# Cross attention of a two-layer decoder: the first query projection and the first key-value tile change places in TensorE's order

## The chip, the cores and the metric

One core of one Trainium2 chip. The metric is the device time of one execution in microseconds (us), as the median of several runs. The trace is that of one profiled execution on the same core.

## The reference, cut to what matters

The program computes a decoder of two layers on a float32 activation `x` of 8 sequences, 256 tokens each, 256 features. Each layer adds to `x` an attention, a second attention and an expert stage, each behind a layer norm. The change concerns the second layer's cross attention alone: 16 query heads, 4 key-value heads, head size 128, a context of 64 tokens per sequence.

```python
q = rms_norm(x @ Wq.T, q_norm_w)                # 16 heads, 256 tokens
kv_in = concatenate([x, ctx], axis=1)           # 256 + 64 = 320 rows
k = rms_norm(kv_in @ Wk.T, k_norm_w)            # 4 key heads
v = kv_in @ Wv.T
q, k = rope(q, pos_q), rope(k, pos_kv)
probs = softmax(q @ k.T * HD**-0.5)             # k, v shared by 4 query heads
x = x + (probs @ v) @ Wo.T
```

## The kernel before, in words

The program runs its stages one behind the other, each in its own block, with the engines' orders written out by hand and semaphores between them. `attention` (from L258) is used twice: for the first layer's self attention (`cross` false) and for the second layer's cross attention (`cross` true).

A unit of work is one key-value head with its four query heads on one sequence. There are 16 units for each of two buffer sets h = 0 and 1, so 32 in all. A unit goes through two halves. The front half projects queries (two tiles of 128 tokens, `project_q`, L386 to L394) and keys and values (three tiles in the cross attention: two of 128 tokens and one of the 64 context rows, `project_kv`, L396 to L404), rotates them, takes their RMS norms, and transposes the queries and keys (`turn_qk`). The back half computes scores of four heads (`score`), their softmax, transposes the probabilities (`turn_probs`), multiplies them with the values (`mix`) and projects back (`give`). A call of `stage(h, front, back)` runs the front half of a unit in set h beside the back half of a unit in the other set, g = 1 - h. `schedule` issues a first stage with no back half, 31 stages with both, and a last one with no front half. Every engine has its own `stage` function, and the order of calls in it is that engine's order of work.

TensorE's order (L464 to L496) in the cross attention is: first query projection; scores of heads 0 and 1; second query projection and key-value tile 0; transposes of probabilities 0 and 1; mixes 0 and 1; scores 2 and 3; key-value tiles 1 and 2; transposes 2 and 3; mixes 2 and 3; `give`; `turn_qk`. Each PSUM set has four banks: the query tiles of a front half take banks 0 and 1, the key-value tiles 2 and 3.

The waits around the change: `score` of head 0 waits for `qk_kept`, which ScalarE signals after copying the transposed queries (`qT`, L657) and keys (`kT`, L658) out of PSUM. `project_q` of tile 0 waits for GpSimd's copy of the input tokens (L358, L360) and for VectorE's add of the previous output (L604). Three signals on `projected` tell VectorE that query tile 0, query tile 1 and all key-value tiles are there.

VectorE's order (L607 to L636): maxima of heads 0 and 1 (L570), normalization of 0 and 1 (L584, L587), copies of a part of the transposed probabilities (L596), rotation of the query tiles (L522 to L524), maxima 2 and 3, normalization of head 2, rotation of the keys (L522 to L524 again), normalization of head 3, two copies, sums of squares (L550, L551), the add of the rotated halves (L540), scaling of the keys (L558, L562), output add (L604). ScalarE's order (L683 to L702): exponentials (L666), copies of transposed probabilities (L673), copies of mixes (L681), and in `keep_v`, once the keys are rotated, squares (L648 to L650) and values (L652, L653), and last `qT` and `kT`. GpSimd takes the inverse root (L366) and the input copies for the next unit. There are no transfers inside the attention.

The self attention runs `project_q` of tile 0 behind scores 0 and 1, and has two key-value tiles, both behind scores 2 and 3.

Of the kernel before, what the change touches and what calls it, by code (L numbers as in the profile page):

```python
# [257 lines left out]
def attention(k, weights, rope, ctx):  # L258
# [9 lines left out]
    cross = ctx is not None  # L268
    scale = float(HD) ** -0.5
    KT = TB + 1 if cross else TB  # L270
# [5 lines left out]
    with ExitStack() as st:  # L276
# [45 lines left out]
        HB = B // 2  # L322


        early = 1 if cross else 0

        def group(u):
            return u // HB
# [16 lines left out]
        def wait_before(eng, sem, value):  # L345

            if not isinstance(value, int) or value > 0:
                eng.wait_ge(sem, value)

        with nc.Block() as block:  # L350
# [32 lines left out]
            def _(pe):  # L383
                pe.wait_ge(weights.loaded, 16 * weights.loads)

                def project_q(h, u, t):  # L386
                    if t == 0:
                        pe.wait_ge(s.xb_ready[h], u + 1)

                        wait_before(pe, s.out_added[h], u)  # L390
                    for c in range(DC):
                        last = nc.tensor.matmul(k.ps[h][:, t, :], xb[h][:, c, t * P:(t + 1) * P],  # L392
                                                wq[:, c, ds(group(u) * (G * HD), G * HD)], start=c == 0, stop=c == DC - 1)
                    last.then_inc(s.projected[h], 1)  # L394

                def project_kv(h, u, tiles):  # L396
                    for t in tiles:
                        o = k.ps[h][0:krows[t], 2 + t // 2, (t % 2) * 2 * HD:(t % 2 + 1) * 2 * HD]
                        for c in range(DC):
                            last = nc.tensor.matmul(o, xb[h][:, c, t * P:t * P + krows[t]],  # L400
                                                    wkv[:, c, ds(group(u) * (2 * HD), 2 * HD)],
                                                    start=c == 0, stop=c == DC - 1)
                    if t == KT - 1:
                        last.then_inc(s.projected[h], 1)  # L404

                def turn_qk(h, u):

                    pe.wait_ge(s.turned_in[h] if cross else s.summed[h], u + 1)
                    pe.wait_ge(s.v_kept[h], u + 1)
                    for hh in range(G):  # L410
                        for t in range(TB):
                            nc.tensor.transpose(slot(h, hh)[:, t * P:(t + 1) * P], t1[h][:, t, hh, :], k.ident[:, :])
                    for t in range(KT):
                        r = krows[t]
                        last = nc.tensor.transpose(k.ps[h][:, 2, t * P:t * P + r], t1[h][0:r, t, G, :],
                                                   k.ident[0:r, 0:r])
                    last.then_inc(s.qk_turned[h], 1)

                def score(h, u, r):
                    if r == 0:  # L420
                        pe.wait_ge(s.qk_kept[h], u + 1)
                    elif r > 1:

                        pe.wait_ge(s.mix_kept[h], u * G + (r - 1))
                    for t in range(TB):
                        nk = NK if cross else (t + 1) * P
                        o = k.ps[h][:, (r % 2) * TB + t, :]
                        last = nc.tensor.matmul(o[:, 0:nk], qT[h][:, r, t * P:(t + 1) * P],  # L428
                                                kT[h][:, 0:nk], start=True, stop=cross)
                        if not cross:  # L430

                            last = nc.tensor.matmul(o[:, t * P:nk], k.identb[:, :],
                                                    k.causb[:, :], start=False, stop=True)
                    last.then_inc(s.scored[h], 1)

                def turn_probs(h, u, r):
                    pe.wait_ge(s.probs_ready[h], u * G + (r + 1))
                    for j in range(KT):
                        w = krows[j]
                        for t in range(TB):  # L440
                            if cross or j <= t:
                                last = nc.tensor.transpose(slot(h, (r % 2) * 4 + pieces[j])[0:w, t * P:(t + 1) * P],  # L442
                                                           probs[h][:, (r % 2) * TB + t, j * P:j * P + w], k.ident[:, :])
                    last.then_inc(s.probs_turned[h], 1)

                def mix(h, u, r):
                    pe.wait_ge(s.probs_kept_a[h], u * G + (r + 1))
                    pe.wait_ge(s.probs_kept_d[h], u * G + (r + 1))
                    for j in range(KT):
                        w = krows[j]  # L450
                        c0 = 0 if cross else j * P
                        last = nc.tensor.matmul(slot(h, (r % 2) * 4 + 3)[:, c0:S], v[h][0:w, j, :],  # L452
                                                pT[h][0:w, r % 2, j, c0:S], start=j == 0, stop=j == KT - 1)
                    last.then_inc(s.mixed[h], 1)

                def give(h, u):
                    pe.wait_ge(s.mix_kept[h], u * G + G)
                    for t in range(TB):
                        for hh in range(G):
                            last = nc.tensor.matmul(slot(h, t), oT[h][:, hh, t * P:(t + 1) * P],  # L460
                                                    wo[:, ds(group(u) * G + hh, 1), :], start=hh == 0, stop=hh == G - 1)
                    last.then_inc(s.out_ready[h], 1)

                def stage(h, front, back):  # L464
                    g = 1 - h
                    if front is not None and cross:
                        project_q(h, front, 0)
                    if back is not None:
                        score(g, back, 0)
                        score(g, back, 1)  # L470
                    if front is not None:
                        if not cross:
                            project_q(h, front, 0)
                        project_q(h, front, 1)
                        if early:
                            project_kv(h, front, range(early))
                    if back is not None:
                        turn_probs(g, back, 0)
                        turn_probs(g, back, 1)
                        mix(g, back, 0)  # L480
                        mix(g, back, 1)
                        score(g, back, 2)
                        score(g, back, 3)
                    if front is not None:
                        project_kv(h, front, range(early, KT))
                    if back is not None:
                        turn_probs(g, back, 2)
                        turn_probs(g, back, 3)
                        mix(g, back, 2)
                        mix(g, back, 3)  # L490
                    if back is not None and cross:
                        give(g, back)
                    if front is not None:
                        turn_qk(h, front)
                    if back is not None and not cross:
                        give(g, back)  # L496
# [1906 lines left out]
def build(nc, ins, out):  # L2403
    with ExitStack() as stack:
        k = Core(nc, ins, out, stack)
        load_constants(k)
        with ExitStack() as st, k.own_semaphores("_0"):
            rope = SelfRope(k, st)
            weights = AttentionWeights(k, ("w0q", "w0kv", "w0o"), st)
            layernorm(k)  # L2410
            attention(k, weights, rope, None)
        layernorm(k)
        with ExitStack() as st, k.own_semaphores("_m"):
            weights = ExpertWeights(k, st)
            set_attention(k)
            routed_experts(k, weights)
        layernorm(k)
        with k.own_semaphores(""):
            delta_attention(k)
        with ExitStack() as st, k.own_semaphores("_1"):  # L2420
            weights = AttentionWeights(k, ("w1xq", "w1xkv", "w1xo"), st)
            rope = CrossRope(k, st)
            layernorm(k)
            attention(k, weights, rope, rope)
        with ExitStack() as st, k.own_semaphores(""):
            k.xn_rows = k.sb("xn_rows", [P, NT, D], F32, st)
            layernorm(k, k.xn_rows)
            sparse_experts(k)
# [83 lines left out]
```

## Time and profile before

| | |
|---|---|
| median of 3 runs | 4484.63 us (4478.69 to 4495.13) |
| profiled execution, its own time | 4505.4 us |
| its span in the trace | 4503.6 us |
| granted TensorE clock over the span | 0.896 |
| busy: TensorE, VectorE, ScalarE, GpSimd | 3543.0, 2730.2, 1614.0, 1555.6 us |

The profile is a page and a packed trace of one execution. Engines: PE is TensorE's matmuls (a transpose is one too), PEld its weight loads, DVE VectorE, ACT ScalarE, POOL GpSimd. A float32 matmul shows as two instructions. The ends of matmuls are modelled, so successive starts are the safer measure of their pace. Lines of the trace such as L428 are lines of the kernel. In the order of time the cross attention lies at about 3050 to 3970 us.

### The profile page before, as it was taken

The page shows a single profiled execution, that of the slowest core. Times are in us where ns is not written, and L with a number is a line of the kernel's source. Part 1 is how long each engine was busy: PE and PEld are TensorE (multiplying, and loading weights), DVE is VectorE, ACT ScalarE, POOL GpSimd, SP SyncE. Part 2 cuts the span into 40 slices and gives each one's busy share as a digit, 9 for nine tenths or more (in the row PEclk, how much of TensorE's full clock was granted, in tenths as well). Part 3 has the DMA queues.
Part 4 walks back from the last instruction along what each step waited for, and adds up shares of the span by engine and source line. Part 5 has one row for each costly group of instructions (what it writes and reads, how often), then busy time and mean ns, then how long its engine had stood idle before and what let it go on. Part 6 is the DMA issues. An engine that isn't in the chain of part 4 may idle for free. (4 is left out here: it accounts for less than half of the span.)

```text
span 4503.6 us, 58245 instructions
## 1 busy us (share of the span) xinstructions
PE 3543.0 (79%) x17574; PEld 2742.3 (61%) x17574; DVE 2730.2 (61%) x7933; ACT 1614.0 (36%) x4118; POOL 1555.6 (35%) x2243
## 2 busy tenths in 40 slices
PE   6999993589577999999999999847999999940320
PEld 4677662455366888888888888735655655530320
DVE  4666652532257888888888888545666666652123
ACT  2434441123234545555555555313444444410100
POOL 0000000058515555555555555501111111117357
PEclk9999995589778999999999999978999999965665
DMA  2000004135411111111111111110000000021340
GB/s 69 0 0 0 0 0 106 63 61 84 85 30 34 29 38 24 38 24 38 28 37 41 24 38 24 19 56 1 0 0 0 0 0 0 0 91 39 100 116 13
DMA packets 225351, 152.21 MB, mean 34 GB/s; under 512 B 125496, under 2 KB 211702, under 8 KB 224096
## 3 DMA queue, kind: packets, MB, share of 16 engines
q1 hardware_dynamic: 192880, 113.99, 9.8%
q0 software_dynamic: 27456, 30.91, 3.7%
q10 hardware_dynamic: 4800, 4.72, 0.3%
q8 instruction: 100, 1.64, 0.1%
q14 instruction: 115, 0.94, 0.1%
HBM read 117.41 MB, written 56.11 MB: 39 GB/s over the span
## 5 line engine op out<-in xcount | busy, mean ns | idle before, releaser
L1869 DVE SCALAR_TENSOR_TENSOR dl_y<-ps,dl_taps,dl_y 128x255 f32<-128x255 f32 (+2 forms) x1536 | 653.0, 475 | 130.6 <-ACT dl_y L1765 126.4
L1600 PE MATMUL ps<-xnT,dl_wkqv 128*128 128x256 f32 x2048 | 544.8, 392 | 29.0 <-DVE dl_lp L1912 23.3
L1600 PEld LDWEIGHTS ps<-xnT,dl_wkqv 128*128 128x128 f32 x2048 | 370.4, 194 | 81.2 <-issue 38.2
L366 POOL TENSOR_TENSOR at_rs<-at_ss,mhalf 128x15 f32<-128x15 f32 x32 | 125.5, 3921 | 745.8 <-DVE at_ss L553 745.8
L1523 POOL TENSOR_TENSOR dl_rn<-dl_n,mhalf 128x4 f32<-128x4 f32 x128 | 173.3, 1354 | 553.0 <-DVE dl_n L1885 553.0
L452 PE MATMUL ps<-at_shared,at_v 128*128 128x256 f32 (+2 forms) x1280 | 315.7, 380 | 4.6 <-ACT at_shared L676 0.2
L1765 ACT ACTIVATE dl_y<-ps,dl_taps 128x256 f32<-128x256 f32 x512 | 260.2, 560 | 106.2 <-PE ps L1600 106.2
L428 PE MATMUL ps<-at_kT,at_qT 128*128 128x320 f32 (+2 forms) x1024 | 271.2, 397 | 2.8 <-ACT at_kT L658 2.8
L1541 POOL TENSOR_TENSOR dl_inv_u<-dl_inv_u,dl_inv_tmp 64x30 f32<-64x30 f32 (+14 forms) x480 | 259.0, 540 | 37.6
L452 PEld LDWEIGHTS ps<-at_shared,at_v 128*128 128x128 f32 (+1 forms) x1280 | 211.1, 190 | 89.3 <-issue 64.0
L392 PE MATMUL ps<-at_wq,at_xb 128*128 (+1 forms) x512 | 246.1, 614 | 4.5 <-POOL at_xb L360 2.4
L442 PE MATMUL ps<-ident,at_probs 128*128 128x128 f32 (+1 forms) x1152 | 173.8, 283 | 96.3 <-DVE at_probs L587 93.1
L460 PE MATMUL ps<-at_wo,at_oT 128*128 (+1 forms) x1024 | 234.8, 382 | 18.7 <-ACT at_oT L681 18.7
L1625 PE MATMUL ps<-dl_wo,dl_z 128*128 128x256 f32 x1024 | 243.2, 380 | 0.0
L1538 POOL TENSOR_TENSOR dl_inv_tmp<-dl_inv_u,dl_inv_a 64x30 f32<-64x30 f32 (+14 forms) x480 | 232.9, 485 | 24.7
L358 POOL COPY at_xb<-xnT 128x512 f32 (+1 forms) x64 | 38.9, 609 | 566.5 <-PE ps L400 561.7
L1773 ACT ACTIVATE dl_z<-dl_y 128x512 f32<-128x512 f32 x256 | 161.5, 631 | 185.2 <-DVE dl_y L1869 185.2
L442 PEld LDWEIGHTS ps<-ident,at_probs 128*128 128x128 f32 (+1 forms) x1152 | 124.1, 135 | 169.5 <-DVE at_probs L587 156.3
L1611 PE MATMUL ps<-dl_z 128*128 128x512 f32 (+1 forms) x512 | 225.4, 523 | 0.0
L460 PEld LDWEIGHTS ps<-at_wo,at_oT 128*128 128x128 f32 x1024 | 189.4, 190 | 54.7 <-issue 27.5
L428 PEld LDWEIGHTS ps<-at_kT,at_qT 128*128 128x128 f32 x1024 | 175.1, 191 | 70.8 <-ACT at_kT L658 13.7
L570 DVE TENSOR_REDUCE at_mx<-ps 128x2 f32<-128x640 f32 x128 | 105.6, 825 | 180.6 <-PE ps L428 177.1
(332 smaller groups left out, 7944.7 us busy)
## 6 DMA issues: line engine op xcount, KB each, us to landing
dl_grow<-decay_rows SPq DMA_DIRECT2D x128, 128.0 KB, 3.0
sp_wgu<-in_w1gu SPq DMA_DIRECT2D x12, 768.0 KB, 10.5
dl_wkqv<-in_w1kqv SPq DMA_DIRECT2D x16, 512.0 KB, 4.9
delta_diag<-dl_lp SPq DMA_DIRECT2D x512, 8.0 KB, 1.5
dl_diag<-delta_diag_tt SPq DMA_DIRECT2D x512, 8.0 KB, 1.7
moe_wgu<-in_w0gu SPq DMA_DIRECT2D x16, 448.0 KB, 10.4
slot_rows<-sp_zero SPq DMA_DIRECT2D x4, 1152.0 KB, 8.1
sp_wd<-in_w1d SPq DMA_DIRECT2D x12, 384.0 KB, 12.0
```

What stands on the lines that cost most here:

```text
L392: last = nc.tensor.matmul(k.ps[h][:, t, :], xb[h][:, c, t * P:(t + 1) * P], wq[:, c, ds(group(u) * (G * HD), G * HD)], start=c == 0, stop= ...
L428: last = nc.tensor.matmul(o[:, 0:nk], qT[h][:, r, t * P:(t + 1) * P], kT[h][:, 0:nk], start=True, stop=cross)
L442: last = nc.tensor.transpose(slot(h, (r % 2) * 4 + pieces[j])[0:w, t * P:(t + 1) * P], probs[h][:, (r % 2) * TB + t, j * P:j * P + w], k.i ...
L452: last = nc.tensor.matmul(slot(h, (r % 2) * 4 + 3)[:, c0:S], v[h][0:w, j, :], pT[h][0:w, r % 2, j, c0:S], start=j == 0, stop=j == KT - 1)
L460: last = nc.tensor.matmul(slot(h, t), oT[h][:, hh, t * P:(t + 1) * P], wo[:, ds(group(u) * G + hh, 1), :], start=hh == 0, stop=hh == G - 1)
L1538: nc.gpsimd.tensor_tensor(tmp, inv_u[:, 0:i, i:i + 1].to_broadcast([GP, i, w]), inv_a[:, i:i + 1, i + 1:Q32].to_broadcast([GP, i, w]), ALU ...
L1541: nc.gpsimd.tensor_tensor(inv_u[:, 0:i, i + 1:Q32], inv_u[:, 0:i, i + 1:Q32], tmp, ALU.subtract)\
L1600: last = nc.tensor.matmul(bank(h, m // 2, (m % 2) * S, (m % 2 + 1) * S), wkqv[h][:, c, m * P:(m + 1) * P], k.xnT[:, c, u.seq * S:(u.seq + ...
L1611: last = nc.tensor.matmul(bank(h, blk, 0, 2 * (S - blk * P)).rearrange("p (a s) -> p a s", a=2), z[h][:, 0, blk * P:(blk + 1) * P], z[h][: ...
L1625: last = nc.tensor.matmul(bank(h, 3, t * D, (t + 1) * D), z[h][:, 2 + m, t * P:(t + 1) * P], wo[h][:, m, :], start=m == 0, stop=m == 1)
L1765: last = nc.scalar.activation(y[h][:, m, :], bank(h, m // 2, (m % 2) * S, (m % 2 + 1) * S), ACT.Identity, bias=taps[h][:, m, KC:KC + 1], s ...
L1869: last = nc.vector.scalar_tensor_tensor(y[h][:, m, back:S], bank(h, m // 2, (m % 2) * S, (m % 2 + 1) * S - back), taps[h][:, m, KC - 1 - b ...
```

## The change

```diff
@@ -322,7 +322,6 @@
         HB = B // 2


-        early = 1 if cross else 0

         def group(u):
             return u // HB
@@ -463,17 +462,12 @@

                 def stage(h, front, back):
                     g = 1 - h
-                    if front is not None and cross:
-                        project_q(h, front, 0)
                     if back is not None:
                         score(g, back, 0)
                         score(g, back, 1)
                     if front is not None:
-                        if not cross:
-                            project_q(h, front, 0)
+                        project_q(h, front, 0)
                         project_q(h, front, 1)
-                        if early:
-                            project_kv(h, front, range(early))
                     if back is not None:
                         turn_probs(g, back, 0)
                         turn_probs(g, back, 1)
@@ -482,7 +476,7 @@
                         score(g, back, 2)
                         score(g, back, 3)
                     if front is not None:
-                        project_kv(h, front, range(early, KT))
+                        project_kv(h, front, range(KT))
                     if back is not None:
                         turn_probs(g, back, 2)
                         turn_probs(g, back, 3)
```

In the cross attention's TensorE order both query projections now stand behind the scores of heads 0 and 1, and all three key-value tiles behind those of heads 2 and 3. The instructions are the same in kind and number, the waits and signals too. The self attention's order stays as it was, and is now the same as the cross attention's up to `give`. The other engines' orders are not touched.

## Rows read from the trace of the kernel before

**Rows 1.** The page, part 2: TensorE's granted clock in 40 slices, in tenths.
```profile
PEclk9999995589778999999999999978999999965665
```

**Rows 2.** Windows: start:end, length, busy us (instructions) of each engine, granted clock.
```profile
3103.00:3950.00 847.00, 771.52 (x3330) 507.65 (x3328) 532.17 (x1410) 356.00 (x931) 140.59 (x88) 1.00 0.00 0
```

**Rows 3.** Source L657 in the cross attention: ns min/median/max, first and last start.
```profile
L657 ACT COPY at_qT<-ps x32: 1012/1012/1012, 3072.7 to 3949.6; 128x1024 f32<-128x1024 f32 x32
```

**Rows 4.** Waits of TensorE, 3074 to 3949.9 us: total, times, longest.
```profile
PE ps L442 <- DVE at_probs L587: 55.5, 93, 1.1
PE ps L460 <- ACT at_oT L681: 17.8, 31, 0.6
PE ps L412 <- DVE at_t L562: 2.8, 16, 0.2
```

**Rows 5.** Timeline of TensorE in a steady stage: start us, busy us, instruction, idle before.
```profile
3528.01 2.32 PE L428 MATMUL ps<-at_kT,at_qT 128*128 128x320 f32 x8
3530.16 1.88 PE L392 MATMUL ps<-at_wq,at_xb 128*128 x4
3531.88 1.03 PE L400 MATMUL ps<-at_wkv,at_xb 128*128 x4
3532.74 0.82 PE L442 MATMUL ps<-ident,at_probs 128*128 128x128 f32 x6
3533.83 0.87 PE L442 MATMUL ps<-ident,at_probs 128*128 128x128 f32 x6 [0.26 <-DVE at_probs L587]
3534.54 3.34 PE L452 MATMUL ps<-at_shared,at_v 128*128 128x256 f32 x12
3537.81 2.42 PE L428 MATMUL ps<-at_kT,at_qT 128*128 128x320 f32 x8
3540.07 2.03 PE L400 MATMUL ps<-at_wkv,at_xb 128*128 x8
3542.53 0.88 PE L442 MATMUL ps<-ident,at_probs 128*128 128x128 f32 x6 [0.43 <-DVE at_probs L587]
3544.50 0.87 PE L442 MATMUL ps<-ident,at_probs 128*128 128x128 f32 x6 [1.10 <-DVE at_probs L587]
```

**Rows 6.** Timeline of ScalarE in the same stage.
```profile
3526.30 1.01 ACT L657 COPY at_qT<-ps 128x1024 f32<-128x1024 f32 x1 [5.57 <-PE ps L415]
...
3533.60 0.59 ACT L673 COPY at_shared<-ps 128x512 f32<-128x512 f32 x1 [0.75 <-PE ps L442]
...
3543.93 1.03 ACT L648 ACTIVATE at_shared<-ps 128x1024 f32<-128x1024 f32 x1
```

**Rows 7.** Timeline of VectorE in the same stage.
```profile
3529.29 0.82 DVE L570 TENSOR_REDUCE at_mx<-ps 128x2 f32<-128x640 f32 x1 [3.72 <-PE ps L428]
...
3541.79 0.68 DVE L587 TENSOR_SCALAR at_probs<-at_probs,at_rden 128x320 f32<-128x320 f32 x2
3542.39 0.42 DVE L522 TENSOR_TENSOR at_t<-ps,rope_ck 128x256 f32<-128x256 f32 x1
...
3543.45 0.21 DVE L524 TENSOR_TENSOR at_t<-ps,rope_sc 64x64 f32<-64x64 f32 x1
...
3543.76 0.68 DVE L587 TENSOR_SCALAR at_probs<-at_probs,at_rden 128x320 f32<-128x320 f32 x2
```

**Rows 8.** Timeline of the last stage, which has no front half.
```profile
3949.55 1.01 ACT L657 COPY at_qT<-ps 128x1024 f32<-128x1024 f32 x1 [5.20 <-PE ps L415]
...
3950.95 2.42 PE L428 MATMUL ps<-at_kT,at_qT 128*128 128x320 f32 x8 [1.43 <-ACT at_kT L658]
3952.33 0.82 DVE L570 TENSOR_REDUCE at_mx<-ps 128x2 f32<-128x640 f32 x1 [3.28 <-PE ps L428]
```

**Rows 9.** Timeline of the first stage, no back half: all key-value tiles in one block.
```profile
3057.01 2.90 PE L400 MATMUL ps<-at_wkv,at_xb 128*128 128x256 f32 x12
...
3059.95 0.42 DVE L522 TENSOR_TENSOR at_t<-ps,rope_ck 128x256 f32<-128x256 f32 x1 [1.38 <-PE ps L400]
```

**Rows 10.** Timeline of the second stage's start: a query projection at the lower clock.
```profile
3072.60 3.72 PE L392 MATMUL ps<-at_wq,at_xb 128*128 128x512 f32 x4
```

## The prediction

> **What bounds the kernel now.** The page comes first: in its 40 slices of 113 us TensorE is granted nearly its full clock through most of this attention, slices 29 to 35 [rows 1]. The windows view of the cross attention's steady part shows TensorE busy for 771.5 of 847.0 us, VectorE 532.2, ScalarE 356.0, at clock 1.00 [rows 2]. So TensorE's queue is the thing to follow, and its idle time is what an order of work can win or lose. The 32 copies of `qT` run from 3072.7 to 3949.6, so a stage takes (3949.6 - 3072.7)/31 = 28.29 us [rows 3]; the sampled steady stage takes 28.24 by the same copy. The waits of TensorE name three kinds of idle time: on normalized probabilities 55.5 us in 93 waits (1.79 a stage), on the kept mix 17.8, on the scaled keys 2.8 [rows 4]. The change moves work around the first kind.
>
> I follow one stage on a clock that starts at T, the start of the `qT` copy at 3526.30 [rows 6]. TensorE's steps [rows 5]: first query projection before T; first scores T+1.71; second query projection T+3.86; key-value tile 0 T+5.58; first transposes of probabilities T+6.44, second T+7.53 (0.26 idle); mixes T+8.24; second scores T+11.51; key-value tiles 1 and 2 T+13.77; third transposes T+16.23 (0.43 idle); fourth T+18.20 (1.10 idle, the largest).
>
> The last wait is a chain through VectorE, to be read in its own rows [rows 7]. It normalizes head 2 from 3541.79, goes straight on to rotate the keys at T+16.09, and only behind that normalizes head 3 from 3543.76. TensorE's fourth transposes wait for that. Whatever delays the key rotation delays head 3's probabilities.
>
> **Part 1: the first query projection goes from ahead of scores 0 and 1 to behind them.** Nothing is added or removed in number: 4 matmuls, no transfer, no new wait. Its two waits (input ready, output added) move with it and were met by its old place. What it loses is its cover. Today it runs while ScalarE copies `qT` and `kT`, which the scores need. The last stage of this attention has no front half, so the trace already shows that stretch without a projection: TensorE idles 1.43 us and scores start 1.40 after the `qT` copy (3950.95 - 3949.55) [rows 8]. Today it is 1.71, so scores start 0.31 sooner. Not all is gain: with no matmul ahead of them their own first one isn't overlapped, and the row maximum starts at T+2.78 there (3952.33 - 3949.55) against T+2.99 today (3529.29 - 3526.30) [rows 7, 8]. I take 0.20 sooner for what follows, so the projections start at T+3.66.
>
> A page bears on a longer gap. The row shows the 8 scores behind the 1.43 us gap taking 2.42 us, the same as scores elsewhere at full clock took with the 0.10 of start-up [rows 5, 8], so I add nothing. The Trainium skill (TensorE: Matmul & The Clock Gate, "Why this matters for your kernels") warns that idle gaps between bursts of matmuls send the clock back to its lower level; by the row this gap doesn't, and if it did the sum would be that of the fourth case below.
>
> **Part 2: key-value tile 0 goes from behind the second query projection to behind scores 2 and 3.** Between scores and first transposes there are now two query projections instead of one and a key-value tile. One query projection takes 3531.88 - 3530.16 = 1.72; tile 0 takes 3532.74 - 3531.88 = 0.86 [rows 5]. First transposes: 3.66 + 2 x 1.72 = T+7.10, 0.66 later than today. Both heads' probabilities are ready before that (they let today's second transposes go at T+7.53, and come 0.2 sooner), so the 0.26 idle is gone. Second transposes follow after 0.71 (the space from transposes to mix today, 3534.54 - 3533.83): T+7.81. The mixes could start at T+8.52, but need ScalarE's copy of the first transposes, which starts 0.86 after them (3533.60 - 3532.74) and takes 0.59 [rows 5, 6]; with 0.06 for the hand-over that is T+8.61, 0.37 later than today. Without the copy it would be 0.28. I take 0.37, since by its own rows the copy ends last, if narrowly.
>
> Scores 2 and 3 and their maxima shift by 0.37; the key-value block now starts at 13.77 + 0.37 = T+14.14, and holds 12 matmuls for 8. The attention's very first stage runs just this block of 12 at full clock: VectorE's key rotation starts 3059.95 - 3057.01 = 2.94 after it begins [rows 9]. So the rotation starts at 14.14 + 2.94 = **T+17.08 instead of T+16.09: 0.99 later**. Head 2 is normalized by T+16.54 (16.17, the end of the two operations from 3541.79, plus 0.37), so VectorE now waits some 0.5 us for tile 0, where before it had no wait at all. Queued behind it: the rotation, head 3's normalization, the last copies, the sums of squares, the adds. TensorE's third transposes start at about T+16.7, 0.5 later, and that is covered; the fourth wait for head 3 and start at T+19.19.
>
> **The tail.** After that every queue carries the 0.99. ScalarE's squares start at 3543.93, 0.28 after the rotation's end (0.21 us operation begun at 3543.45, in the same stretch), since a copy is ahead of them [rows 6, 7]; they slip 0.7 to 0.8, which VectorE's sums, already 0.99 late, hide. GpSimd's inverse root starts from those sums and sets the scaled keys; the TensorE wait on them is small [rows 4], so output projection and key chain are level and both late. No slack there to give anything back. No queue of SyncE or of transfers is passed.
>
> **Sum.** 31 stages have both halves (32 copies less the first stage, whose order stays; the last stage has no projections): 31 x 0.99 = +30.7 us. The same by TensorE's idle time: +1.43 at the start, -0.26 and -0.43 at transposes, more than today's 1.10 at the fourth. Against the profiled execution of 4505.4 us that gives 4536; it is 20.8 above the median of the runs shown, 4484.6, to which I add the same: **4515 us**, +0.68%. About 0.5% is what a measurement of this kernel can tell from no change, 22.4 us or 0.72 a stage.
>
> Bounds of the uncertain terms, per stage: hand-over and copy 0.28 to 0.45; start of scores gain 0.1 to 0.31; block to rotation 2.9 to 3.0. Together 0.8 to 1.15, so 25 to 36 us.
>
> **Rivals.**
> *The delay at the fourth transposes is absorbed.* Only TensorE's balance up to the mixes counts, 0.37 x 31 = 11.5: 4496 us. For it: 1.10 of idle sits in front of the fourth transposes, and TensorE itself is late by only 0.5 there. Against: that idle is VectorE's, queued behind the very rotation that moves.
> *Not slower: stalls removed exceed the one made.* The 1.79 a stage on probabilities [rows 4] all vanish behind longer blocks, and 1.43 appears [rows 8]: -0.36 x 31 = -11, 4473 us. It decides if VectorE's rotation can still start by T+16.09, that is if the key-value block ends nearly 1 us sooner than I have it. Only idle time that I haven't seen inside TensorE's stream could give that.
> *Cover lost in full.* The stalls on probabilities all stay, because scores, maxima and exponentials move with the shift, and the start gap comes whole: 1.43 x 31 = 44: 4529 us.
> *The clock falls in the new gap.* At the lower level of 1.2 GHz the four projection matmuls took 3.72 us at 3072.60 [rows 10] against 1.88 [rows 5], 1.84 more; once a stage, 57 us above the forecast: 4572. The scores of rows 8 speak against it.
>
> **Numbers.** Forecast 0.76, absorbed 0.12, not slower 0.04, cover lost 0.06, clock 0.02. The forecast's own range with 5 to 8 us of scatter between runs is 4503 to 4526; reaching a little towards 4496 and 4529 gives 4500 to 4527. Slower by over 0.5%: 0.84 of cases, less what scatter around 22.4 may take from the forecast, 0.79. Within: 0.19. Faster: the -11 case is -0.25% and would need scatter as well, 0.02.
>
> **What the changed profile would show.** Right: the `qT` copies 29.2 us apart; TensorE waiting about 1.4 us for `kT` in each stage; first and second transposes with no idle; a new VectorE wait of some 0.5 us on the key-value matmuls ahead of the key rotation; fourth transposes waiting 1.4 to 1.6 instead of 1.10; self attention and all other stages unchanged. Wrong: spacing under 28.9, or no VectorE wait before the rotation, or matmuls longer at a lower granted clock.

## The result and the profile after

The changed kernel takes 4528.23 us in the median of 4 runs (4522.94 to 4532.68). The kernel before, with one more run beside it, takes 4489.88 (4478.69 to 4495.35). The ratio is 1.009, with a 95% interval of 1.0075 to 1.0105: slower by 34 to 47 us, where 30.7 were forecast and the range ended at 4527.

The first view is the one that gave the length of a stage: the copies of `qT` (rows 3 before; here also those of the self attention, so the last start is the one to read) and the timeline of the cross attention's first, last and two steady ones.

```profile
L651 ACT COPY at_qT<-ps x32: 1012/1012/1012, 3066.0 to 3982.2; 128x1024 f32<-128x1024 f32 x32
...
3127.26 1.01 ACT L651 COPY at_qT<-ps 128x1024 f32<-128x1024 f32 x1 [5.57 <-PE ps L414]
3156.55 1.01 ACT L651 COPY at_qT<-ps 128x1024 f32<-128x1024 f32 x1 [5.57 <-PE ps L414]
```

Over 31 stages that is (3982.2 - 3066.0)/31 = 29.55 us instead of 28.29: 39.4 us in all, as much as the medians differ. The two profiled spans alone differ by only 17.6 (4521.2 and 4503.6), since 6.7 us fewer passed before the first of these copies and 15.1 fewer behind the last, in work that the change doesn't touch. The stage's length, and not the span of one execution, is what experiments are read by below.

The waits of TensorE show the same kinds as [rows 4], with one new (waiter and releaser, total us, times, longest).

```profile
PE ps L441 <- DVE at_probs L581: 44.2, 31, 1.4
PE ps L427 <- ACT at_kT L652: 42.9, 30, 1.4
PE ps L459 <- ACT at_oT L675: 17.7, 31, 0.6
PE ps L411 <- DVE at_t L556: 2.8, 16, 0.2
```

Waits on normalized probabilities went from 93 to 31: two of three are gone, as forecast, and the one left is longer (1.44 us for 1.10). Each stage now waits 1.43 us for `kT` (the view's window leaves one of the 31 out).

A steady stage, as [rows 5] and [rows 7] showed it, with T = 3600.64:

```profile
3602.04 2.42 PE L427 MATMUL ps<-at_kT,at_qT 128*128 128x320 f32 x8 [1.43 <-ACT at_kT L652]
3604.29 3.60 PE L391 MATMUL ps<-at_wq,at_xb 128*128 x8
3607.73 1.47 PE L441 MATMUL ps<-ident,at_probs 128*128 128x128 f32 x12
3609.22 3.44 PE L451 MATMUL ps<-at_shared,at_v 128*128 128x256 f32 x12
3612.59 2.42 PE L427 MATMUL ps<-at_kT,at_qT 128*128 128x320 f32 x8
3614.85 2.90 PE L399 MATMUL ps<-at_wkv,at_xb 128*128 x12
3617.68 0.88 PE L441 MATMUL ps<-ident,at_probs 128*128 128x128 f32 x6
3617.88 0.42 DVE L516 TENSOR_TENSOR at_t<-ps,rope_ck 128x256 f32<-128x256 f32 x1 [0.62 <-PE ps L399]
3619.99 0.87 PE L441 MATMUL ps<-ident,at_probs 128*128 128x128 f32 x6 [1.44 <-DVE at_probs L581]
```

The reader can lay the forecast's steps beside it, in us after T:

| step | forecast | measured |
|---|---|---|
| scores 0 and 1 | 1.40 | 1.40 |
| query projections | 3.66 | 3.65 |
| first transposes | 7.10 | 7.09 |
| mixes | 8.61 | 8.58 |
| key-value block of 12 | 14.14 | 14.21 |
| key rotation on VectorE | 17.08 | 17.24 |
| fourth transposes | 19.19 | 19.35 |

Steady stages in the loop take 29.38 us. But two of them take 31.07, and the attention's first two-sided stage 31.98 (29.97 before). In these the scores behind the new gap look like this:

```profile
3156.24 0.27 PE L414 MATMUL ps<-ident,at_t 64*128 64x64 f32 x1
3157.94 4.11 PE L427 MATMUL ps<-at_kT,at_qT 128*128 128x320 f32 x8 [1.43 <-ACT at_kT L652]
3161.89 3.60 PE L391 MATMUL ps<-at_wq,at_xb 128*128 x8
```

4.11 us for the 8 matmuls that otherwise take 2.42. The windows view (busy us of each engine, then the granted clock) gives 0.72 around it and 1.00 around the same place of the stage that follows the second such case:

```profile
3156.00:3162.00 6.00, 4.57 (x13) 2.81 (x12) 0.98 (x2) 2.00 (x5) 0.00 (x0) 0.72 0.00 0
...
3601.00:3605.00 4.00, 2.96 (x10) 2.00 (x11) 1.49 (x3) 1.51 (x4) 0.00 (x0) 1.00 0.00 0
```

The clock fell to its lower level of 1.2 GHz after the gap, for most of the length of the scores: the granted clock was 1.00 up to the end of the gap, 0.50 in the microseconds from 3159 and 3160, and 1.00 again from 3162. Before it fell, TensorE had made the transposes of queries and keys from 3155.00, after a short wait of 0.25 us, and then stood idle for 1.43. The 31 stages add up: 31 x 1.14 = 35.3, two falls of 1.69 = 3.4, and the first two-sided stage's further 0.9, less 0.2 for the two stages that took 29.29.

### The profile page after: what moved, and what is told of

The parts are those of the page before. It is cut to its first block and busy times, and to the rows that moved or that the text cites. A ratio compares the mean times of both kernels' runs of the same rounds, so it can differ in the third digit from the quotient of the medians.

```text
span 4521.2 us, 58259 instructions
## 1 busy us (share of the span) xinstructions
PE 3536.1 (78%) x17574; PEld 2737.4 (61%) x17574; DVE 2729.6 (60%) x7933; ACT 1615.3 (36%) x4118; POOL 1557.6 (34%) x2243
```

## The experiments

In the results below a stage is the most frequent distance between two copies of `qT`. Ratios are to the kernel before, run beside each experiment.

**Part 1 alone.**

```diff
                         project_q(h, front, 1)
+                        if cross:
+                            project_kv(h, front, range(1))
...
-                        project_kv(h, front, range(KT))
+                        project_kv(h, front, range(1 if cross else 0, KT))
```

> The changed kernel with key-value tile 0 put back behind the second query projection: part 1 of the change alone (first query projection behind scores 0 and 1). My steps: scores at T+1.40, projections at T+3.66, tile 0 at T+7.1, first transposes at T+7.96 instead of T+6.44, mixes about 1.3 later, and all behind them too, since the later waits on VectorE keep their size (0.43 and 1.10). Stage 28.24 + 1.3 = about 29.55 us, so +40 us on the kernel before, as much as the whole change or more: the parts do not add. The rival (absorbed at the fourth transposes) expects a stage of at most 28.9. If the clock falls at times in the new gap of 1.43 us, one to three stages of this run are about 1.7 us longer than the rest.

Measured: stage 29.53 us, two stages of 31.2; ratio 1.0094 (1.0072 to 1.0115).

**Part 2 alone.**

```diff
-        early = 1 if cross else 0
+        early = 0
```

> The kernel before with all three key-value tiles behind scores 2 and 3: part 2 of the change alone; the first query projection keeps its cover. My steps: scores at T+1.71 as before, first transposes wait for normalized probabilities and start near T+6.33, mixes T+8.24 and second scores T+11.51 as before, key-value block of 12 from T+13.77, key rotation 3.03 behind it at T+16.80 instead of T+16.09. Stage 28.24 + 0.71 = 28.95 us, +22 us. The rival that the first projection's lost cover is all of the cost expects 28.24, no change. There is no gap ahead of the scores, so no stage should show a lower clock.

Measured: stage 28.94 us, no longer one but the first; ratio 1.0042 (1.0022 to 1.0061). Losing the first projection's cover alone costs 1.29 us a stage, moving tile 0 alone 0.70, both together 1.14. They do not add, because the second part takes 0.86 us out of the very stretch that the first makes longer, the one up to the first transposes. Part 2 costs something without any gap ahead of the scores, so TensorE's lost cover isn't all of it.

**The order on VectorE, in the changed kernel.**

```diff
                         norm_probs(g, back, 2)
+                        if cross:
+                            norm_probs(g, back, 3)
                     if front is not None:
                         rotate(h, front, TB)
                     if back is not None:
-                        norm_probs(g, back, 3)
+                        if not cross:
+                            norm_probs(g, back, 3)
```

> The changed kernel with VectorE's normalization of head 3 ahead of the key rotation, in the cross attention. If the fourth transposes are late because head 3's normalization is queued behind a rotation that waits for key-value tile 0, their idle of 1.44 us goes, and they follow the third transposes at T+17.75 instead of T+19.35. The other leg of the tail, rotation, squares, sums, inverse root and scaled keys, moves little: rotation at T+17.6, ScalarE's squares 0.4 later, its copy for the last mix 0.4 later, sums at about T+20.4. So the stage gets only 0.2 us shorter, 29.2, and the transposes of queries and keys wait for the scaled keys by 0.5 us or more. The rival that TensorE's own length sets the stage expects 28.0 to 28.3.

Measured: stage 29.30 us, five of 30.97 to 30.99 (and 32.36 first); ratio 1.0098 (1.0076 to 1.0119). Waits of TensorE in it:

```profile
PE ps L427 <- ACT at_kT L655: 42.9, 30, 1.4
PE ps L451 <- DVE at_shared L590: 22.5, 31, 0.7
PE ps L459 <- ACT at_oT L678: 17.7, 31, 0.6
PE ps L411 <- DVE at_t L556: 8.0, 30, 0.4
PE ps L451 <- ACT at_shared L670: 7.3, 31, 0.2
```

The wait on probabilities is gone, so it was the queue behind the rotation that made it. Hardly anything is won (29.30 us for 29.38): 0.73 us of it came back ahead of the mixes, for VectorE's copy of head 2's probabilities (L590), which is queued behind the rotation as well, and 0.24 for ScalarE's copy. I had expected 29.2 and had not seen the first of these waits. The sums over queries and keys still start where they must, behind the squares.

**The gap filled with repeated work.** Nothing is left out; key-value tile 0 is projected twice.

```diff
                     g = 1 - h
+                    if front is not None and back is not None and cross:
+                        warm(h, front)
```

where `warm` waits for the input and the output add and makes tile 0's four matmuls into its own place.

> The changed kernel with key-value tile 0 projected once more at the head of each stage, ahead of scores 0 and 1 (4 matmuls, 0.86 us, the result is overwritten later by the same values). It fills more than half of the 1.43 us gap and takes nothing from the scores, which still start at T+1.40. If the few stages of 31.07 us in the changed kernel are TensorE's clock falling in that gap, they are gone and all steady stages take 29.38; about 3 to 5 us less in all. If they are chance and have nothing to do with the gap, they stay. If an uncovered first query projection costs anything beyond the gap itself, the steady stage changes too.

Measured: steady stages 29.29 ahead of the loop and 29.38 in it, none of 31; the first two-sided one 30.38 for 31.98. The copies run from 3065.7 to 3977.1, so the attention is 4.8 us shorter than in the changed kernel (911.4 for 916.2), and TensorE's wait there is 11.1 us in 30 stages. Ratio 1.006 (1.0041 to 1.0079). In this trace no steady stage shows a fall. By itself that is weak, since two kernels further below keep the full gap and have no fall either. What ties the lower clock to the gap is its place: in four traces there are 14 steady stages with longer scores (4.06 to 4.11 us), and in each of them the scores stand right behind 1.43 us of idle time. The rest of the cost is not the idle time itself: with TensorE at work in 0.86 of the 1.43 us, the steady stage is the same.

**The loop written out.** All units of the cross attention in Python's loop instead of `Fori`.

> The changed kernel with the cross attention's loop over units written out, so that no address or wait value is computed in registers. In the changed kernel VectorE's key rotation starts 2.93 us after the first key-value matmul in the three stages ahead of the loop and 3.03 in the loop, and the stages take 29.29 and 29.38. If the 0.09 is register work that VectorE can only do once its wait has ended, all stages take 29.29 here, and the rotation starts 2.93 behind the block everywhere. The rival (it comes from TensorE's side, or from the weights' place in memory) expects 29.38 to stay. Should the stages show other waits, of instructions not there in time, then writing out costs more than it tells.

Its timeline in the middle of the attention:

```profile
3652.47 2.90 PE L404 MATMUL ps<-at_wkv,at_xb 128*128 128x256 f32 x12
...
3655.40 0.42 DVE L521 TENSOR_TENSOR at_t<-ps,rope_ck 128x256 f32<-128x256 f32 x1 [0.53 <-PE ps L404]
```

2.93 us from block to rotation and 29.29 for a stage, throughout. So the 0.09 comes with the loop, in which addresses and wait values are computed in registers. The kernel before, where VectorE doesn't wait at this place, takes 28.23 to 28.25 us a stage ahead of the loop and in it. Whether the time is VectorE's own or that of TensorE's signal is not separated by this run. Five stages of 30.9 to 31.0, with scores of 4.06 to 4.11 us behind the gap, ate more than that won: the copies run from 3075.3 to 3994.4, 919.1 us for 916.2. The whole took 4551.02 in its single run, which says little.

**Tile 0 as the cover.** Where the first projection stood before, tile 0; both projections behind the scores.

```diff
                     g = 1 - h
+                    if front is not None and cross:
+                        warm(h, front)
+                        project_kv(h, front, range(1))
...
-                        project_kv(h, front, range(KT))
+                        project_kv(h, front, range(1 if cross else 0, KT))
```

Here `warm` holds only the two waits.

> The changed kernel with key-value tile 0 moved to the head of the stage, ahead of scores 0 and 1 (the place that the first query projection had), the other two tiles behind scores 2 and 3, both query projections behind scores 0 and 1. By my steps the gap is filled by 0.86 us of needed work, scores start at T+1.40, the second key-value block has 8 matmuls again from T+14.21, so the key rotation no longer waits for it and starts behind head 2's normalization at T+16.53, 0.44 later than in the kernel before. Stage 28.24 + 0.44 = 28.68 us, 0.70 shorter than the changed kernel, and none at a lower clock. The rival that the first projection's own cover is what counts expects it near 29.4.

Measured: stage 28.67 us, none longer but the first; ratio 1.0026 (1.0014 to 1.0038). TensorE and VectorE in it:

```profile
3532.93 2.04 PE L399 MATMUL ps<-at_wkv,at_xb 128*128 x8
3535.25 0.42 DVE L523 TENSOR_TENSOR at_t<-ps,rope_ck 128x256 f32<-128x256 f32 x1
3535.39 0.87 PE L445 MATMUL ps<-ident,at_probs 128*128 128x128 f32 x6 [0.42 <-DVE at_probs L588]
3537.36 0.87 PE L445 MATMUL ps<-ident,at_probs 128*128 128x128 f32 x6 [1.10 <-DVE at_probs L588]
```

The rotation waits for nothing again, and both of the old waits, 0.43 and 1.10, stand where they stood, only 0.43 us later. This separates the two costs of the change. Of its 1.14 us a stage, 0.43 is what reaches the second scores by way of the longer stretch between the first scores and the transposes (0.34 of it is there when the mixes start); 0.71 is the key-value block of 12.

**Both legs of the tail.** With the queue behind the rotation shown as the cause, I shortened it in the kernel before. VectorE's and ScalarE's parts of the edit, shortened (the `if cross` and the lines at the old places are left out):

```diff
                         keep_mix(g, back, 0)
+                        square_q(h, front, 0); square_q(h, front, 1)
                         keep_mix(g, back, 1)
...
                         rotate(h, front, 1)
+                        rms_queries(h, front, 0); rms_queries(h, front, 1)
...
                         norm_probs(g, back, 2)
+                        norm_probs(g, back, 3)
                         rotate(h, front, TB)
...
                         keep_probs(g, back, 2)
+                        keep_probs(g, back, 3)
                         keep_v(h, front)
```

`square_q` and `rms_queries` are ScalarE's squares and VectorE's sums of one query tile; `rms` then sums the keys alone.

> The kernel before with both legs of the tail shortened, in the cross attention: VectorE normalizes head 3 ahead of the key rotation, ScalarE copies head 3's transposed probabilities ahead of its work on keys and values, and the squares and sums of the queries (ScalarE 2 x 0.56 us, VectorE 2 x 0.64) are taken tile by tile behind each query rotation, where both engines idle ahead of scores 2 and 3. TensorE's order is that of before. I expect the 1.10 us ahead of the fourth transposes to fall to about 0.3, the sums of the keys to end some 0.8 us sooner, and the stage to go from 28.24 to about 27.5: 23 us less than before, ratio 0.995. If only the length of TensorE's stream counted, the same; if the maxima of heads 2 and 3 are held up by the new sums, nothing is gained.

> The changed kernel with the same rework of VectorE's and ScalarE's orders as f1_both_legs. If the change costs what it costs because the key rotation and what is queued behind it are moved, then with those legs shortened the fourth transposes follow the third at T+17.8, and the remaining difference to f1_both_legs is TensorE's: 1.43 of gap, less the 0.26 and 0.43 that vanish and 0.3 at the fourth transposes, so 0.5 to 0.9 us a stage. Stage about 28.2, near the kernel before.

Measured: f1_both_legs 28.04 to 28.11, ratio 0.9985 (0.9975 to 0.9995); f2_both_legs_changed 28.48 to 28.55, ratio 1.0015 (1.0005 to 1.0026). I had expected 27.5 and 28.2. The timeline of f1_both_legs has the reason:

```profile
3504.88 0.87 PE L444 MATMUL ps<-ident,at_probs 128*128 128x128 f32 x6 [0.32 <-DVE at_probs L596]
...
3505.93 0.74 DVE L605 COPY at_shared<-ps 64x256 f32<-64x256 f32 x2
...
3506.48 3.41 PE L454 MATMUL ps<-at_shared,at_v 128*128 128x256 f32 x12 [0.73 <-ACT at_shared L691]
```

The transposes come in time, and the mixes wait 0.73 us. The view names ScalarE's copy, but ScalarE's copy of head 2's transposes had long been done; VectorE's two copies, merged in the second row, start only at 3505.93, behind the rotation. It is the same wait as in the third experiment.

**The copy ahead of the rotation, too.** In both, VectorE's `keep_probs(g, back, 2)` goes ahead of `rotate(h, front, TB)`.

> f1_both_legs with VectorE's copy of head 2's transposed probabilities ahead of the key rotation. In f1_both_legs the fourth transposes came 1.20 us behind the third, but the mixes then waited 0.73 us for that copy, queued behind the rotation. With it ahead, mixes follow the fourth transposes after 0.71, 0.8 to 0.9 us sooner; the rotation starts 0.4 later, the sums end at the same time as there. Stage 28.08 - 0.85 = about 27.25 us, 31 us less than the kernel before, ratio about 0.993. If the leg over the sums was level with the mixes already, at most 0.1 is gained.

> f2_both_legs_changed with the same copy ahead of the key rotation: TensorE's order of the changed kernel with VectorE's and ScalarE's of f3_copy2_first. Mixes up to 1.1 us sooner, but the key rotation is still 1.2 us later than in the kernel before and now sets the stage through squares, sums and inverse root: 27.7 to 28.2 us, below the kernel before's 28.24 and 0.4 to 0.9 above f3_copy2_first.

Measured: f3_copy2_first, stage 27.23 us, 4459.35 in the median for the kernel before's 4488.94 beside it, ratio 0.9933 (0.9919 to 0.9947): 30 us faster, and the best of all. f4_copy2_changed, with TensorE's changed order, 27.89, ratio 0.9974 (0.9965 to 0.9983). f3_copy2_first's mixes follow without a wait:

```profile
3510.69 0.87 PE L444 MATMUL ps<-ident,at_probs 128*128 128x128 f32 x6 [0.33 <-DVE at_probs L596]
3511.40 3.34 PE L454 MATMUL ps<-at_shared,at_v 128*128 128x256 f32 x12
```

With these orders on the other engines TensorE's change costs 0.66 us a stage instead of 1.14.

## Why the prediction was right and wrong

**Right: the mechanism and its path.** "0.99 later" for the key rotation, and everything queued behind it late by as much, is what the trace after shows, step by step, within 0.16 us. The new wait of VectorE was put at some 0.5 us and is 0.53 to 0.62. The 0.26 and 0.43 went, the fourth transposes' wait came to 1.44. The two separate parts (29.55 and 28.95 expected, 29.53 and 28.94 measured) and tile 0 as the cover (28.68 and 28.67) confirm the same steps from other sides.

**Right: the rivals refused.** "Absorbed" needed a stage of 28.6, "not slower" a rotation by T+16.09; it came at T+17.24. "Cover lost in full" left all stalls standing; two of three went. That its 4529 us lies next to the measured 4528.2 is luck: it asked for 1.43 us a stage, 1.14 were measured, and the level from which it was counted has moved by 5.3 us.

**Wrong by size: the 0.99 a stage, which measured 1.15 on the path and 1.14 in the stage.** Two terms made it. The bound of 2.9 to 3.0 from the key-value block to the rotation was read from the attention's first stage [rows 9]. That one stands ahead of the loop; in the loop it is 3.03, as the written-out version shows by going back to 2.93. The other is the step from ScalarE's copy to the second scores. I took the copy's end for the start of the mixes and passed the shift of 0.37 on unchanged; it was 0.44 at the second scores (T+11.95 for T+11.51). From the mixes' start to the second scores it now takes 3.37 us (3612.59 - 3609.22) instead of 3.27 (3537.81 - 3534.54). The mixes' first weight load shows why, before and after:

```profile
3534.43 0.73 PEld L452 LDWEIGHTS ps<-at_shared,at_v 128*128 128x128 f32 x4
3609.22 0.73 PEld L451 LDWEIGHTS ps<-at_shared,at_v 128*128 128x128 f32 x4 [0.29 <-ACT at_shared L667]
```

Before, it starts 0.11 us ahead of the first mix, beside the last transposes. Now it waits for the copy and starts with the first mix. From weight load to second scores it is 3.38 and 3.37 us, so the mixes themselves are no longer; the 0.10 is the start-up that I had counted for the first scores (2.42 for 2.32) and left out here. The mixes came 0.03 sooner than forecast. Together 0.15 x 31 = 4.7 us.

**Wrong: "so I add nothing" for the clock.** I took one gap of 1.43 us, in the last stage, for all. In the changed kernel's trace the clock fell behind that gap in two of the steady stages, at 1.69 us each, and the first two-sided stage lost 0.9 more; in the trace with 0.86 us of the gap filled the attention was 4.8 us shorter. My fourth case was there, but as once in every stage, so it looked refuted by a single row. The Trainium skill (TensorE: Matmul & The Clock Gate, "Why this matters for your kernels") warns against idle gaps between bursts of matmuls, and means longer ones than this. The trace shows the fall behind a gap of 1.43 us as well, in some stages, at 1.7 us a time; the measurement decides.

**The level.** I added to 4484.6; with the fourth run the kernel before stands at 4489.9. Of the 13.2 us between 4515 and 4528.2 that is 5.3. The other 8 are what the attention's 39.4 us have over 30.7, within the scatter of the medians: 4.7 of mis-sized terms and some 4 of clock. My range ended 1 us short of the result. It had room for the scatter of runs and for the terms' bounds, but gave the clock no part.

**Open.** Why the falls come where they do. Kernels with the full gap had two (the changed one, part 1 alone), five (VectorE's order changed, written out), or none (f2_both_legs_changed, f4_copy2_changed) beside the first stage; those with less than 0.5 us of it had none. The falls are not scattered. With VectorE's order changed they stand 177.5 us apart each time, which is six stages, and so do the first four of the written-out kernel. And all 14 stand in stages in which TensorE had also waited, for 0.15 to 0.28 us, for the scaled keys just ahead of the transposes that precede the gap. In the changed kernel and in part 1 alone only about every second stage has that wait; in the two kernels without a fall no steady stage has it. That points to the two waits together with only transposes between them, but no run moved one of them alone, and most stages with both waits show no fall. I didn't try to move a stage's length in small steps either.

## What to carry to other kernels

Follow the change on one steady stage with a clock of its own, engine by engine, to the first queue in which something else stands behind the moved work; here that was VectorE, and a filler moved on TensorE cost what VectorE had queued behind its last piece. Work that fills a wait belongs where the wait is longest and its consumer latest; an order that fills one wait and lets two signals come late can lose more than it fills. When a wait is taken away, look at once for the next instruction that the same queue makes late: here the normalization, then a copy, and only with both moved did the stage get shorter.

## What I had not expected of the hardware

A gap of 1.43 us in TensorE's work was enough at times to bring its clock down for one group: 4.11 us for 2.42, at a granted clock of 0.72 over 6 us; in most stages the same gap did nothing, and no fall came without a second, shorter wait (0.15 to 0.28 us) ahead of the transposes before it. A semaphore wait in a loop with register addresses cost 0.09 us more from the last matmul to VectorE's start than the same wait written out (3.03 and 2.93 from the block's start), which is only seen where the engine really waits. And a weight load that had to wait for its operand, instead of running beside the transposes ahead of it, put 0.10 us on the way from the mixes' start to the next scores (3.37 us for 3.27), although no idle time of the matmuls shows there.
